# Finishing four batches without the last half expert's rows, and writing those rows over them

## The reference, cut to what matters

```python
xn = layernorm(x)
s = attn(xn)                # chunked linear attention, 16 heads, chunks of 128;
                            # o * rsqrt(mean(o*o) + 1e-6) * norm_weight, then @ Wo.T
g = silu(ffn(xn))           # each of 8 experts takes its top 128 tokens of each batch:
                            # out[idx] += gating * (silu(x_e @ Wg) * (x_e @ Wu)) @ Wd
out = x + s * g
```

## Time and profile before

| | us |
|---|---|
| median of 3 runs | 838.71 (837.76 to 840.04) |
| the profiled execution, its own time | 838.68 |
| its span, first to last instruction | 836.9 |
| PE busy in the span | 783.8 |
| DVE busy in the span | 541.6 |
| ACT busy in the span | 508.7 |
| POOL busy in the span | 413.8 |

### The profile page before, as it was taken

How to read it: one execution, slowest core, us unless ns; L and a number is a source line. 1 busy time by engine, 2 the same in 40 slices (tenths; PEclk the granted TensorE clock), 3 DMA queues, 4 the chain that set the end, 5 groups by cost and what they waited for, 6 DMA issues and landing times.

```text
span 836.9 us, 17482 instructions
## 1 busy us (share of the span) xinstructions
PE 783.8 (94%) x6460; PEld 678.3 (81%) x6460; DVE 541.6 (65%) x1024; ACT 508.7 (61%) x1184; POOL 413.8 (49%) x362
## 2 busy tenths in 40 slices
PE   7638999999999999999999999999999999999990
PEld 5526788888888888888888888888888888888880
DVE  6885756666566675666556675576556675565567
ACT  5695755766466665666466655665566655655455
POOL 7767636464255616463355626463364625471311
PEclk9778999999999999999999999999999999999995
DMA  8289898676567857676566757576667758670788
GB/s 279 93 284 226 302 372 214 171 197 196 150 155 192 178 178 165 160 196 193 162 148 193 187 167 161 165 195 190 177 145 189 192 165 230 167 179 16 219 254 288
DMA packets 137637, 160.85 MB, mean 192 GB/s; under 512 B 11856, under 2 KB 108624, under 8 KB 137552
## 3 DMA queue, kind: packets, MB, share of 16 engines
q1 hardware_dynamic: 124832, 142.91, 56.3%
q0 software_dynamic: 12288, 16.79, 12.5%
q10 hardware_dynamic: 432, 0.04, 0.0%
HBM read 117.48 MB, written 42.21 MB: 191 GB/s over the span
## 4 chain that ended last, share of the span: by engine, by line
PE 87%; DMA 3%; SPq 2%; POOL 1%; DVE 1%; issue 1%; ACT 1%; ACTq 0%; DVEq 0%; POOLq 0%
PE y_ps L1699 22%; PE g_ps L1666 21%; PE up_ps L1666 21%; PE m_ps L1542 5%; PE a_ps L1614 4%; PE o_ps L1650 3%; PE m_ps L1596 3%; PE m_ps L1560 2%; PE m_ps L1589 2%; DMA qk_dram<-qk_r 1%; PE o_ps L1639 1%; PE m_ps L1570 1%; SPq L739 1%; DMA ffn_dram<-y_sb,idx_all 1%; DMA w_raw<-w_experts 1%; SPq L695 1%
## 5 line engine op out<-in xcount | busy, mean ns | idle before, releaser
L1666 PE MATMUL up_ps<-xgt,w_r 128*128 128x512 f32 (+1 forms) x792 | 205.8, 395 | 0.0
L1699 PE MATMUL y_ps<-w_r,hid_r 128*128 128x256 f32 x1536 | 205.1, 282 | 0.7 <-DVE hid_r L1493 0.7
L1666 PE MATMUL g_ps<-xgt,w_r 128*128 128x512 f32 (+1 forms) x792 | 201.0, 389 | 3.3 <-ACT xgt L1046 1.8
L1699 PEld LDWEIGHTS y_ps<-w_r,hid_r 128*128 128x128 f32 x1536 | 192.5, 190 | 1.4 <-DVE hid_r L1493 1.0
L1467 DVE SCALAR_TENSOR_TENSOR sg<-sg,g_ps 128x512 f32<-128x512 f32 x123 | 84.2, 684 | 159.9 <-ACT sg L1211 159.9
L887 POOL TENSOR_TENSOR w_r<-w_raw,w_r 128x768 fp32r<-128x768 f32 x64 | 123.1, 1925 | 103.3 <-ACT w_r L1111 103.1
L1666 PEld LDWEIGHTS up_ps<-xgt,w_r 128*128 128x128 f32 x792 | 140.2, 188 | 26.8
L1666 PEld LDWEIGHTS g_ps<-xgt,w_r 128*128 128x128 f32 x792 | 137.7, 189 | 26.1 <-issue 3.6
L1211 ACT ACTIVATE sg<-g_ps 128x512 f32<-128x512 f32 (+1 forms) x132 | 77.1, 584 | 117.0 <-PE g_ps L1666 116.5
L916 POOL DMA_INDIRECT ffn_dram<-y_sb,idx_all x64 | 102.9, 1608 | 64.5 <-DVE y_sb L1369 49.0
L882 POOL TENSOR_SCALAR_AFFINE_SELECT lb_row<-lb_row 128x1024 f32<-128x1024 f32 x62 | 75.8, 1233 | 84.0 <-DMA lb_row<-lb_tiles 83.8
(11 more groups left out here) (246 smaller groups left out, 1021.2 us busy)
## 6 DMA issues: line engine op xcount, KB each, us to landing
lb_row<-lb_tiles SPq DMA_DIRECT2D x62, 512.0 KB, 4.5
w_raw<-w_experts SPq DMA_DIRECT2D x64, 384.0 KB, 3.7
qk_dram<-qk_r SPq DMA_DIRECT2D x32, 512.0 KB, 4.5
k_st<-qk_dram SPq DMA_DIRECT2D x96, 128.0 KB, 3.6
arena<-qk_dram SPq DMA_DIRECT2D x192, 64.0 KB, 3.0
x_all<-x SPq DMA_DIRECT2D x8, 512.0 KB, 9.7
xn_dram<-x_all SPq DMA_DIRECT2D x8, 512.0 KB, 6.6
e_row<-lb_tiles SPq DMA_DIRECT2D x64, 64.0 KB
```

The lines of the kernel that those rows point to most:

```text
L1666: mm = pe.matmul(bank[:, 0:width(n)], w_r[:, m, a, at:at + P], xgt[:, b, k, tokens], start=(j == 0 and k == 0), stop=(j == len(passes) - 1 ...
L1699: mm = pe.matmul(y_ps[:, j, :], hid_r[p][:, a, (j - first_tile) * P:(j - first_tile + 1) * P], w_r[:, m, b, DOWN:DOWN + D], start=(m == 0 ...
```

## The change

Batches are finished in the order 4, 5, 6, 7, 0, 1, 2, 3 (`FINISH`). Batches 4 to 7 are finished from `ffn_dram` as it is after half expert 13, that is without the last half expert, in steps 128 to 139. The last half expert's 512 rows are not scattered into `ffn_dram`. Instead POOL gathers, for the same row numbers, the rows of `x`, of `ffn_dram`, of `s` and the factors `r` (four gathers each, `gather_rows`); DVE adds the gated `y_ps` to the gathered sums (`row_total`), ACT takes Silu (`silu_row`), DVE multiplies by `r` and `s` and adds `x` (`row_result`), and POOL writes the rows over the stored result (`write_rows`), after the batches' own stores have landed. For the gathers `r1` is stored to a new `r_dram` by `store_r`, 28 columns of 128 numbers and later 4. The norm's factors are now made on DVE alone: a first value from the number's bits and three Newton steps, in two parts: token tiles 0 to 27 in steps 120 to 123, tiles 28 to 31 in steps 129 and 130. Silu replaces tanh for the units from step 128 on (before: from 131 on), which saves one DVE instruction each there. Tables `ACT_LATE`, `LATE_BETWEEN` and `DVE_LATE` place the finishing work in the steps.

```diff
+    r_dram = nc.dram_tensor("r_dram", [B * N, 1], F32, kind="Internal").ap()
...
-    SILU = TS + 3 - AHEAD
...
+    SILU = TS - AHEAD
...
+    FINISH = (4, 5, 6, 7, 0, 1, 2, 3)
+    SOON = 3
...
+    SEED = 1.8369137e-20
+    R_STEPS = 12
+    R_PARTS = (slice(0, (B - 1) * TPB), slice((B - 1) * TPB, NT))
...
+    ACT_LATE = {TS: ((4, "silu", 0), (4, "silu", 1)), TS + 1: ((5, "weigh", 0), (5, "silu", 0)),
+                TS + 2: ((5, "silu", 1), (6, "weigh", 0)), TS + 3: ((6, "silu", 0), (6, "silu", 1)),
+                TS + 4: ((7, "silu", 0),), TS + 5: ((7, "silu", 1),), TS + 6: ((0, "silu", 0),), TS + 7: ((0, "silu", 1),),
+                TS + 8: ((1, "silu", 0),), TS + 9: ((0, "row", 0), (1, "row", 0)), TS + 10: ((1, "silu", 1),),
+                TS + 11: ((2, "silu", 0),), TS + 12: ((2, "silu", 1), (3, "silu", 0), (3, "silu", 1))}
+    LATE_BETWEEN = {TS + 2: (4, 512, 1024), TS + 5: (6, 0, 256), TS + 6: (6, 512, 768), TS + 7: (6, 768, 1024),
+                    TS + 8: (7, 0, 256), TS + 9: (7, 256, 512), TS + 10: (7, 512, 768), TS + 11: (7, 768, 1024)}
+    DVE_LATE = {TS: ((4, "weigh", 0, 512),), TS + 1: ((4, "weigh", 512, 1024), (4, "add", 0, 512)),
+                TS + 2: ((5, "scaled", 0, 512),), TS + 3: ((5, "scaled", 512, 1024), (5, "add", 0, 1024), (6, "scaled", 0, 512)),
+                TS + 4: ((6, "scaled", 512, 1024),), TS + 5: ((6, "add", 256, 512),), TS + 6: ((7, "weigh", 0, 512),),
+                TS + 7: ((7, "weigh", 512, 1024),), TS + 9: ((0, "rows", 0, 0),), TS + 10: ((1, "rows", 0, 0),),
+                TS + 11: ((0, "weigh", 0, 512),), TS + 12: ((0, "weigh", 512, 1024),)}
+    SCALED = (5, 6, 3)
...
+        row_s = [e_row[:, :, :].rearrange("p k n -> p (k n)")[:, t * D:(t + 1) * D] for t in range(TPB)]
+        row_r = [peak[:, t:t + 1] for t in range(TPB)]
...
+                    sp.wait_ge(r_step, R_STEPS * (part + 1))
+                    tiles = R_PARTS[part]
+                    sp.dma_start(r_dram.rearrange("(t p) o -> p (t o)", p=P)[:, tiles], r1[:, tiles],
+                                 allow_slow_non_contiguous=True).then_inc(r_out[part], 16)
...
+                    if u == TS - 11:
...
+                        for n in FINISH[:SOON]:
                             fetch_s(n)
+                    if u == TS - 4:
+                        store_r(0)
+                    if u == TS - 2:
+                        sp.wait_ge(scattered, 16 * TPB * (2 * E - 2))
+                        for n in FINISH[:SOON]:
+                            fetch_f(n)
+                        sp.wait_ge(inter_done, (TPB - 1) * (B - 1))
+                        sp.wait_ge(m_done, order["u", B - 1, 1] + 1)
+                        sp.wait_ge(e_done, TS - 2)
+                        for n in FINISH[:SOON]:
+                            fetch_x(n)
                     if 10 <= at <= 13 and b + 1 < B:
...
+                    if u == TS + 1:
+                        sp.wait_ge(av_done, NT)
+                        fetch_f(FINISH[SOON])
                         sp.wait_ge(inter_done, B * (TPB - 1))
                         sp.wait_ge(e_done, TS)
                         sp.wait_ge(m_done, order["x", E - 1, 3] + 1)
-                        for n in range(F_EARLY):
+                        for n in FINISH[SOON:]:
...
                     if u == TS + 3:
+                        fetch_s(FINISH[SOON])
+                        store_r(1)
...
-                    if u == TS + 6:
-                        fetch_s(B - 1)
-                        sp.wait_ge(av_done, NT)
-                        for n in range(F_EARLY, B):
...
                         load_lb((u + 4) // 2)
+                for n in FINISH[:-1]:
+                    store_out(n)
+                store_last(FINISH[-1])
+                sp.wait_ge(o_out, 16 * (TPB + 1))
                 for n in range(2):
-                    sp.wait_ge(dn_done, XQ + MID + n + 1)
-                    sp.wait_ge(last_out[n], 16)
-                    fetch_f(F_EARLY + n)
-                for n in range(3):
-                    store_out(n)
-                sp.wait_ge(dn_done, XS)
...
+                    pool.indirect_dma_start(
+                        out=tile[t], out_offset=None, in_=source,
+                        in_offset=bass.IndirectOffsetOnAxis(ap=idx_all[:, E - 1, TPB + t:TPB + t + 1], axis=0)).then_inc(landed, 16)
...
+                    pool.wait_ge(o_pair[t // 2], 32)
+                    pool.wait_ge(row_done, 2 * t + 2)
+                    pool.indirect_dma_start(
+                        out=out[:, :], out_offset=bass.IndirectOffsetOnAxis(ap=idx_all[:, E - 1, TPB + t:TPB + t + 1], axis=0),
+                        in_=row_f[t], in_offset=None).then_inc(rows_out, 16)
...
+                    if u == TS - 6:
+                        for n_parts in range(2):
+                            pool.wait_ge(qk_out[n_parts], 16 * 2 * B)
+                        for t in range(TPB):
+                            gather_rows(row_x, x, t, row_in_soon)
+                    if u == TS - 4:
+                        pool.wait_ge(scattered, 16 * TPB * (2 * E - 2))
+                        for t in range(TPB):
+                            gather_rows(row_f, ffn_dram, t, row_in_soon)
+                    if u == TS - 2:
+                        pool.wait_ge(qs_done, B)
+                        pool.wait_ge(tot_set, B)
+                        for half in range(2):
+                            pool.wait_ge(s_out[half], 16 * 2 * (B - 1))
+                        pool.wait_ge(r_out[0], 16)
+                        for t in range(TPB - 1):
+                            gather_rows(row_s, s_dram[0:(B - 1) * N, :], t, row_in_soon)
+                            gather_rows(row_r, r_dram[0:(B - 1) * N, :], t, row_in_soon)
+                    if u == TS + 4:
+                        for half in range(2):
+                            pool.wait_ge(s_out[half], 16 * 2 * B)
+                        pool.wait_ge(r_out[1], 16)
+                        gather_rows(row_s, s_dram, TPB - 1, row_in_late)
+                        gather_rows(row_r, r_dram, TPB - 1, row_in_late)
+                    if u == TS + 9:
+                        write_rows(0)
+                        write_rows(1)
...
+                write_rows(2)
+                write_rows(3)
+                pool.wait_ge(rows_out, 16 * TPB)
...
+                def silu_row(t):
+                    act.wait_ge(row_sum, t + 1)
+                    act.activation(row_f[t], row_f[t], ACT.Silu).then_inc(row_silu, 1)
...
-                    if u == TS + 2:
-                        act.wait_ge(r_step, 1)
-                        act.activation(r0[:, :], ms[:, :], ACT.Abs_reciprocal_sqrt).then_inc(r_step, 1)
-                    if u >= TS + 5:
...
-                    if F_EARLY <= f < B - 1:
-                        for h in range(2):
+                    for f, what, h in ACT_LATE.get(u, ()):
+                        if what == "silu":
...
-                    at = slice(h * 512, (h + 1) * 512)
-                    act.activation(f_at[B - 1][:, at], f_at[B - 1][:, at], ACT.Silu).then_inc(g2_done, 1)
+                        elif what == "weigh":
+                            weigh_state(f)
+                        else:
+                            silu_row(f)
+                silu_row(2)
+                silu_row(3)
+                weigh_state(3)
...
+                def row_total(t):
+                    dve.wait_ge(dn_done, XQ + MID if t < 2 else XS)
+                    if t == 0:
+                        dve.wait_ge(row_in_soon, 16 * (4 * TPB - 2))
+                    dve.scalar_tensor_tensor(out=row_f[t], in0=y_ps[:, t, :], scalar=gate_all[:, E - 1, TPB + t:TPB + t + 1],
+                                             in1=row_f[t], op0=ALU.mult, op1=ALU.add).then_inc(row_sum, 1)
+                def row_result(t):
+                    if t == TPB - 1:
+                        dve.wait_ge(row_in_late, 32)
+                    dve.wait_ge(row_silu, t + 1)
+                    dve.scalar_tensor_tensor(out=row_f[t], in0=row_f[t], scalar=row_r[t], in1=row_s[t],
+                                             op0=ALU.mult, op1=ALU.mult).then_inc(row_done, 1)
+                    dve.wait_ge(row_done, 2 * t + 1)
+                    dve.tensor_tensor(row_f[t], row_f[t], row_x[t], ALU.add).then_inc(row_done, 1)
...
+                def mean_squares(part):
+                    dve.tensor_scalar(ms[:, R_PARTS[part]], o_ps[:, D + R_PARTS[part].start:D + R_PARTS[part].stop], 1.0 / D, RMS_EPS,
+                                      ALU.mult, ALU.add).then_inc(r_step, 1)
...
+                    if 0 in steps:
                         dve.wait_ge(r_step, at + 1)
-                        dve.tensor_tensor(nw[:, :], nw[:, :], ms[:, :], ALU.mult).then_inc(r_step, 1)
+                        dve.tensor_scalar(r0[:, cols].bitcast(I32), ms[:, cols].bitcast(I32), 1, 0x7fffffff,
...
                         dve.wait_ge(r_step, at + 2)
...
```

(46 more changed lines are left out.)

191 lines of the change are left out of this document (93 added, 98 removed).

## The result

| | before | changed |
|---|---|---|
| median | 838.24 (837.33 to 840.04, 4 runs) | 852.26 (851.35 to 855.78, 4 runs) |
| ratio to before | | 1.0169 [1.0153, 1.0184] |
| span of the profiled execution | 836.9 | 849.6 |

What follows compares the result with a forecast made beforehand. PE alone bounds the kernel until the last step, then a 19.3 tail leaves it nearly idle. Span 836.9 - 5.6 (tail) + 0.8 (PE late) - 0.2 (overlaps) = 831.9; with 1.78 over span, 833.7; range 831.8 to 836.8.

Steps and rivals of the forecast that it cites:

- The tail: DVE's queue behind the last product into `hid_r`: 13.7 against 19.3 before, so 5.6 less.
- PE 0.8 late: DVE's added work in steps 130 to 132 makes PE 0.8 late, neither made up nor growing in steps 133 to 139.
- The early norm: Eleven small DVE instructions in steps 121 to 123 (2.4) push step 124's products back by 0.7 at most; costed at nothing.
- POOL's masks: Second mask, behind four gathers, ends at 761.9; ACT's exponentials reading it started at 762.44: costs nothing, by 0.5.
- The last store: From DVE's last add to the end of the span, kept at 3.75 as before the change.
- The store of r: 28 columns, 3584 packets of 4 bytes issued at 759.0: 15.9 at SP's 60 ns a packet, landing 774.9; PE waits nothing.
- The loads of `ffn_dram` and `x` for three batches come behind it: Behind the store of r, 10.1 at 312 GB/s, to 785.0; DVE waits about 1, inside step 129's idle time.
- Rival A: Slower: store of r holds POOL and, through the last sum of squares, PE; up to 849.4; chance 0.07.
- point of decision: Rival A eats the whole gain if the store of r takes 22 or more, 88 ns a packet.
- B: The written rows end last, if a landing takes over 10.6: 834 to 837; chance 0.04.
- C: DVE fuller than counted in steps 133 to 139: with PE's lag 3 instead of 0.8, 835.9; chance 0.11.
- D: PE loses nothing and the last store lands in 3.4: 832.5, down to 831.5 with spread; chance 0.08.

Runs made afterwards that it cites:

- changed_again: The changed kernel once more, unchanged, on another chip beside the kernel before: 853.0, ratio 1.0171; its profiled execution took 858.0.
- packed_again: packed once more, unchanged, on the same chip as changed_again: 832.92, ratio 0.9934.
- best_again: packed with half of batch 5's product moved to step 129 and ACT multiplying r into s for batches 1 and 2, second run: 831.14, ratio 0.9914.
- packed: The changed kernel, but r stored as one run of 112 bytes per partition, later one of 16, gathered by places worked out in step 28: 832.15, ratio 0.9928.
- dummy28_wait: The kernel before plus an unread store of 3584 4-byte packets in step 124; SP waits for its landing, then issues a small store: 839.12, ratio 1.0.
- packed_idle0: packed with an unneeded store of 28 columns in 4-byte packets (3584) beside its first store of r: 847.84, one run.
- packed_idle1: packed with an unneeded store of 4 columns in 4-byte packets (512) beside its second store of r: 840.2, one run.

## Why the prediction was wrong, step by step

- **The tail, 13.7:** right. 13.66 in the changed kernel, 13.67 in changed_again (840.05 to 853.72), and 13.66 in packed_again.
- **PE 0.8 late from DVE's work in steps 130 to 132:** right, 0.82 and 0.83, and it neither grew nor was made up. best_again shows that it was DVE: with one product moved out of step 130 the lag is 0.3, and with ACT's share of batches 1 and 2 the tail is 12.8.
- **The early norm and POOL's masks, at nothing:** right in packed_again, which has no wait there.
- **The last store, 3.75:** it was 2.5, in the changed kernel and in packed_again. It made packed 1.2 faster than the sum.
- **The store of r, 15.9 to its landing:** the landing was mis-sized only a little, 18.4 (16.7 to 19.2 in other runs), though by an argument that does not hold. SP's mean of 60 ns a packet is time of the DMA engines; these took 7.7 ns a packet in dummy28_wait, and the rest is spent behind them.
- **"The loads of `ffn_dram` and `x` for three batches come behind it, 6 x 0.52 MB at the 312 GB/s of a full stretch":** this is the step that failed. The sum treated the store as time on a queue, and gave the loads behind it full speed and SP's issues no cost. Instead the core's DMA traffic ran at 8 to 53 GB/s from 764 until the store landed (changed_again), the loads of `ffn_dram` took 20.3 instead of 6.3, and SP, whose issues stretched too, fell behind by over 10 for all that came after. In the changed kernel it was busy issuing these six loads until 779.8 (765.5 in packed_again); in changed_again, where the store was issued 3.7 later than the sum has it, the last of them, due at 785.0, held DVE until 794.5.
- **The second store:** the sum priced the 28 columns of step 124 and left out the 4 columns (512 packets) that follow in step 131. It landed in 10.1 and 11.7, the loads of batches 0 to 3 behind it in 13.5 and 15.0. The largest single loss stands here, 10.7 in the changed kernel and 13.9 in changed_again, but only part of it is this store's: these loads were also issued late through the first one, and packed_idle0 and packed_idle1 each lose about 7 at this place alone.
- **Steps 124 and 125:** the sum had no loss there; the changed kernel's execution has 7.3. Its cause stays open. It is not what makes the change slow: changed_again has none of it and takes 853.0.
- **Rival A** named the right instruction and a time near the result, 849.4, which is luck: its road carries little of the loss. POOL's sum cost PE nothing in the changed kernel and 2.6 in changed_again, where the store landed 19.2 after its issue; by the rival's own sum, with 17.2 free, that costs 2.0, so its price is right. Its point of decision, 22 for the landing, was never reached; the loss came by the loads, for which no rival stood.
- **B, C and D** did not decide anything. C's lag was 0.8.
- The rule on writes below 512 bytes (the Trainium skill, "DMA: Bandwidth & Descriptors", Specifications) spoke for the slow side, and the store was slow; but packed's runs of 112 bytes are below it too and landed in 1.4 to 2.0. The rule alone does not tell these apart; the runs do. No run shows whether the engines read before they write here.

The best version measured is best_again's, 831.14, against 838.69 of the kernel before on that chip. It does not beat it everywhere: on two other chips the same kernel took 841.7, through the stops. packed took 832.2 and 832.9 on two chips, neither of which showed stops in steps 124 to 126 in any kernel; what it takes on one that does was not tried.

## What to carry to other kernels

Don't cost a store of many tiny packets as time on its queue: ask what else of the core reads or writes memory until it lands, give that traffic next to nothing until then, and let the issuing queue fall behind by as much. Lay the data out in runs per partition instead and pay for the places on an engine with slack; here seven small instructions bought 20 us. A store whose own landing nobody needs can still be the dearest instruction of a stage, and a short wait on a load ahead of an engine's everyday work (ACT's Silu ahead of the gates) passes it on to all.
